# A graph network's streaming stage: target columns read from PSUM, and one PSUM region for the third norm's transposed sums

## What is computed

```python
loop = jnp.arange(n)
row_f = jnp.concatenate([row, loop]); col_f = jnp.concatenate([col, loop])
ew_f = jnp.concatenate([edge_weight, jnp.ones((n,))])
deg = segment_sum(ew_f, col_f, num_segments=n)
dinv = jnp.where(deg > 0, rsqrt(deg), 0.0)
norm = dinv[row_f] * ew_f * dinv[col_f]
out = segment_sum((x @ conv_w)[row_f] * norm[:, None], col_f, num_segments=n) + conv_b
x = layernorm(x + out)
```

## Time and profile before

| | us |
|---|---|
| median of 3 runs | 4627.14 |
| lowest, highest | 4626.38, 4638.19 |
| the profiled execution | 4627.41 |
| its span in the trace | 4625.4 |
| streaming stage in it (first spread at 3134.1, last sums in `acc` at 3461.2) | 327 |

### The profile page before, as it was taken

How to read it: one execution, slowest core, us unless ns; L and a number is a source line. 1 busy time by engine, 2 the same in 40 slices (tenths; PEclk the granted TensorE clock), 3 DMA queues, 4 the chain that set the end, 5 groups by cost and what they waited for, 6 DMA issues and landing times.

```text
span 4625.4 us, 66668 instructions
## 1 busy us (share of the span) xinstructions
PE 3383.2 (73%) x22549; PEld 2235.1 (48%) x22549; DVE 2339.7 (51%) x5589; ACT 1342.3 (29%) x3152; POOL 2432.0 (53%) x2486
## 2 busy tenths in 40 slices
PE   4988888886677766774333333337878999999998
PEld 3654545544455444543223232237874555555554
DVE  7755555555566655655555555557881121111112
ACT  1333233232222222223444444447771000000000
POOL 5777777775777777776777777772330000000000
PEclk7999999998888888886555555558999999999999
DMA  4343334443333333334777777778877777777776
GB/s 127 117 132 121 123 122 133 134 126 104 97 100 93 101 101 100 102 98 133 199 198 199 198 199 198 199 199 321 286 255 289 287 284 276 275 290 283 285 286 227
DMA packets 510752, 855.11 MB, mean 185 GB/s; under 512 B 111438, under 2 KB 290298, under 8 KB 510309
## 3 DMA queue, kind: packets, MB, share of 16 engines
q1 hardware_dynamic: 343350, 542.83, 33.4%
q0 software_dynamic: 87808, 179.98, 15.3%
q10 hardware_dynamic: 79248, 127.90, 7.6%
HBM read 632.93 MB, written 217.55 MB: 184 GB/s over the span
## 4 chain that ended last, share of the span: by engine, by line
POOL 49%; PE 31%; issue 16%; DMA 1%; ACT 1%; DVE 1%; ACTq 0%; POOLq 0%; SPq 0%; DVEq 0%
POOL big L853 32%; POOL big L877 16%; PE psS L1945 11%; PE psA L1945 11%; PE psS L1596 4%; PE psA L1825 1%; PE ps L1891 1%; PE ps L1882 1%; ACT big L1279 1%; PE ps L1526 1%; DMA big<-A_rows 0%; PE psA L1631 0%; PE ps L1465 0%; PE ps L1668 0%; DMA xw_rows<-big 0%
## 5 line engine op out<-in xcount | busy, mean ns | idle before, releaser
L853 POOL DMA_INDIRECT big<-ht_rows,reli x784 | 785.4, 1002 | 269.8 <-issue 238.6
L853 POOL DMA_INDIRECT big<-xw_rows,srci x784 | 775.2, 989 | 271.3 <-issue 238.7
L877 POOL DMA_INDIRECT big<-axt_rows,srci x784 | 746.5, 952 | 262.3 <-issue 238.5
L1596 PE MATMUL psS<-big 128*128 128x128 f32 x3136 | 507.8, 330 | 300.8 <-DMA big<-ht_rows,reli 291.2
L1596 PEld LDWEIGHTS psS<-big 128*128 128x128 f32 x3136 | 476.5, 240 | 368.9 <-DMA big<-ht_rows,reli 326.8
L933 POOL TENSOR_TENSOR xsb<-xsb,l3b2r 128x896 f32<-128x896 f32 x6 | 12.5, 2078 | 1114.4 <-DMA xsb<-x_keep 1114.4
L1945 PE MATMUL psS<-big,xsb 128*128 128x448 f16 x1372 | 485.2, 354 | 17.4 <-DMA big<-A_rows 17.4
L1945 PE MATMUL psA<-big,xsb 128*128 128x448 f16 x1372 | 485.1, 354 | 0.0
L1945 PE MATMUL psS<-big,acc 128*128 128x448 f16 x1372 | 483.8, 353 | 0.0
L1945 PE MATMUL psA<-big,acc 128*128 128x448 f16 x1372 | 483.8, 353 | 0.0
L1757 PE MATMUL ps<-identh,xsb 128*128 128x128 bf16 x784 | 101.4, 311 | 513.8 <-DVE xsb L2444 513.8
(11 more groups left out here) (301 smaller groups left out, 5067.3 us busy)
## 6 DMA issues: line engine op xcount, KB each, us to landing
big<-A_rows SPq DMA_DIRECT2D x112, 2744.0 KB
A_rows<-xsb ACTq DMA_DIRECT2D x196, 416.0 KB, 2.7
xg_rows<-big SPq DMA_DIRECT2D x98, 512.0 KB, 3.8
big<-xg_rows SPq DMA_DIRECT2D x98, 512.0 KB, 4.0
marks_rows<-big SPq DMA_DIRECT2D x98, 354.0 KB
big<-marks_rows SPq DMA_DIRECT2D x98, 354.0 KB, 5.6
big<-srcq_list SPq DMA_DIRECT2D x98, 256.0 KB
ht_rows<-big ACTq DMA_DIRECT2D x28, 512.0 KB, 3.0
```

The costliest lines, as they stand in the source:

```text
L853: pool.indirect_dma_start(ring[g % len(ring)][:, j * D:(j + 1) * D], None, table[:, :], bass.IndirectOffsetOnAxis(ap=lists[:, g * TPG + j: ...
L877: pool.indirect_dma_start(wide[g % NS][:, j, :], None, axt_rows[:, :], bass.IndirectOffsetOnAxis(ap=srci[:, g * TPG + j:g * TPG + j + 1], ...
L1596: m = pe.matmul(psS[b][:, 0:P], rows[b][:, j * P:(j + 1) * P], marks[b][:, j * P:(j + 1) * P], start=(j == 0), stop=(j == TPG - 1))
```

## The change

Four edits. ACT copies `dstf` once into `ps4[:, 1024:1808]`, between the last clearing of degree sums and the loop, after a wait on `d_v`. DVE waits for that copy before its loop, and its marks take the targets from the copy instead of from `dstf`; node numbers still come from SBUF. The transposed sums of all chunks now lie in `ps4[:, 0:896]`, so that `turn_own(c)` waits until chunk c-1, not c-2, has been normalised. `turned_rows(c)`, used in a branch that this input does not take, keeps the two regions under a new name.

```diff
-        def own_sums(c):
+        own_sums = ps4[:, 0:CW]
+        targets = ps4[:, 1024:1024 + NG * TPG]
+
+        def turned_rows(c):
             return ps4[:, c % 2 * 1024:c % 2 * 1024 + CW]
...
             zero_degrees(NCE - 1)
+            act.wait_ge(d_v, 3)
+            act.copy(targets, dstf[:, :]).then_inc(k_ready, 1)
...
             def turn_own(c):
-                if c >= 2:
-                    pe.wait_ge(n_xn, c + (N3["xn0"] - 1))
+                if c:
+                    pe.wait_ge(n_xn, c + N3["xn0"])
                 pe.wait_ge(n_st, c + (N3["xn0"] + 1))
                 for k in range(CB):
-                    m = pe.transpose(own_sums(c)[:, k * P:(k + 1) * P], stT[:, k * P:(k + 1) * P], ident[:, :])
+                    m = pe.transpose(own_sums[:, k * P:(k + 1) * P], stT[:, k * P:(k + 1) * P], ident[:, :])
...
+            dve.wait_ge(k_ready, 4)
+
             def row_marks(b, base, w, pair):
                 dve.tensor_tensor(tiles(marked[b]), iota[:, window(base, w)].unsqueeze(1).broadcast_to([P, TPG, P]),
-                                  columns(dstf, pair, b), ALU.is_equal).then_inc(r_oh[b], 1)
+                                  columns(targets, pair, b), ALU.is_equal).then_inc(r_oh[b], 1)
...
-                step(dve.tensor_tensor(blocks(y[:, :]), blocks(own_sums(c)), per_node(dinv[:, c * CB:(c + 1) * CB]), ALU.mult))
+                step(dve.tensor_tensor(blocks(y[:, :]), blocks(own_sums), per_node(dinv[:, c * CB:(c + 1) * CB]), ALU.mult))
```

More of the change, by code:

```diff
@@ L1283, in turned_back @@
                 act.wait_ge(N3["t2"], c + 1)
-                act.copy(acc[:, c * CW:(c + 1) * CW], own_sums(c)).then_inc(N3["eva"], 1)
+                act.copy(acc[:, c * CW:(c + 1) * CW], turned_rows(c)).then_inc(N3["eva"], 1)
             def store_rows(c):
@@ L1840, in turn_final @@
                 for k in range(CB):
-                    m = pe.transpose(own_sums(c)[:, k * P:(k + 1) * P], X[:, c * CW + k * P:c * CW + (k + 1) * P], ident[:, :])
+                    m = pe.transpose(turned_rows(c)[:, k * P:(k + 1) * P], X[:, c * CW + k * P:c * CW + (k + 1) * P], ident[:, :])
                 m.then_inc(N3["t2"], 1)
```

## The result

| | before | after |
|---|---|---|
| median of 12 runs, us | 4627.80 | 4619.42 |
| lowest, highest | 4621.32, 4638.19 | 4612.39, 4624.60 |
| span of the profiled execution | 4625.4 | 4616.8 |
| first copy of sums at | 3144.95 | 3147.93 |
| from the first to the last copy of sums (98 copies) | 315.25 | 302.93 |

The ratio is 0.9977, with a 95% interval of 0.9969 to 0.9986: 0.23% faster. By the medians that is 8.4 us, by the means (4629.2 and 4618.8) 10.4, where 15.7 were forecast.

What follows compares the result with a forecast made beforehand. DVE, PE and ACT take turns at being late in the streaming stage, with ACT gapless in undisturbed groups. 14.2 + 1.5 = 15.7 us off 4627.41 gave 4611.7 us; range 4606 to 4624, a gain of 3 to 21.

Steps and rivals of the forecast that it cites:

- The bound: Streaming stage: ACT works without a gap at 2.53 us a group, DVE has some 0.2 us reserve; other groups took longer.
- The lock on the marks: DVE's marks wait for POOL instructions, 19.6 us beyond the median; 5.4 hidden, so removing it saves 14.2 us.
- The masks: ACT's staging copy and PE's seven transposes lengthen slots anyway, hiding 2.3 and 1.4 us of the long marks.
- The mark's own duration: DVE's mark with targets in PSUM: 1217 ns against 1216, taken as nothing, within +/-1 us in all.
- The copy, the wait and the single region: ACT's added copy, DVE's wait for it and PE's wait before its transposes: cost nothing.
- One long instruction stays: DVE's L2556, two SBUF inputs, still meets POOL's L893 in chunk 3; no size given.
- PE's clock: Third norm, chunks 1 and 4: shorter pauses without long marks shorten PE's slow two-slot stretches, 1.5 us.
- right: Signs: marks' mean 1210 to 1225 ns, longest below 1300, slots behind L893 2.5 us, stage 13 to 18 us shorter.
- hidden: Sign of a wrong forecast: marks are short, but the stage shortens by less than 10 us.
- More is hidden than I see: Rival, chance 0.14: half of the 14.2 us in the stage is lost, the clock gives nothing; 4620 us.
- The lock did not stay: Rival, chance 0.06: DVE's marks still hold the second port, or POOL stops their write; 4627 us.
- PSUM did not slow the marks: Rival, chance 0.06: the repeated PSUM column makes DVE's marks slower; at 0.5 us a mark, 4647 us.

Runs made afterwards that it cites:

- x_region: The changed kernel with its marks reading dstf from SBUF again, copy and single region kept; 4624.4 us, ratio 0.9995 to the kernel before.
- x_before2: The kernel before, run again with no edit; 4630.1 us, ratio 1.0003.
- x_after2: The changed kernel, run again with no edit; 4618.6 us, ratio 0.9980 to the kernel before.
- x_one_later: The changed kernel with only chunk 1's own_scaled step of POOL one group later; 4614.1 us, ratio 0.9967 to the kernel before.
- x_tiny_sbuf: The kernel before with POOL's three steps cut from 896 columns to 7, so the result is not right; 4608.5 us, ratio 0.9966.
- x_shift2: The changed kernel with POOL's three steps per chunk moved away from the third norm, run a second time; 4610.7 us, ratio 0.9960 to the kernel before.
- x_shift: The changed kernel with POOL's three steps per chunk moved to where DVE has no third-norm piece; 4609.9 us, ratio 0.9965 to the kernel before.

## Why the prediction was right or wrong

**The bound** was read rightly. Undisturbed groups stayed at 2.51 to 2.55 us; what shrank were long ones.

**The lock on the marks: right, and its size nearly so.** DVE's marks lost 138.7 - 118.6 = 20.1 us, of which 19.6 were named. Outside the third norm's busy slots (21 to 25, 35 to 37, 49, 50, 63, 64, 77, 78, 91, 92, and the first) the other 80 slots shrank by 14.2 us together, where I had put 11.4 of the term, with 2.8 in the third norm's. That this equals the whole term is chance. The 19 of the 80 slots that had held a long mark shrank by 10.5 us; the other 3.7 came from slots without one, 1.25 of it from slot 94, which comes up again below. The masks were mostly as read: slot 72, which a staging copy stretches, had a mark 0.72 us too long and lost nothing of its 3.32; slot 30 went from 3.62 to 3.32, slot 75 from 3.68 to 3.00. (The long marks are 22, not 21: the last of all, at 3456.2, took 1478 ns beside a POOL add; its slot was 1.78 us and is 1.79.) One mask was read too large: the slots of PE's transposes that I had at 3.25 us without a long mark (33, 61 and 89) fell to 3.00 too.

**The mark's own duration: right.** 1211 ns for the 1216 before; the earlier trace rows had 1217. The 65 ns of the prediction's estimate from the Trainium skill do not show.

**The copy, the wait and the single region: right**, nothing that shows, by x_region.

**"One long instruction stays": this step failed.** I had looked for DVE's two-input instructions that could meet POOL, and found L2556. It stayed, at 2.49 us. L2311, now L2317, with one SBUF input, was not on the list, since it took 0.17 us in every instance of the first trace. It takes 1.5 to 1.9 us when POOL gets there first. The second trace of the unchanged kernel shows one too, so the change did not make this collision possible:

```profile
3358.02 2.09 POOL L899 TENSOR_TENSOR big<-xsb,cbr 128x896 f32<-128x896 f32 x1
3358.23 1.91 DVE L2311 TENSOR_SCALAR stat<-stat 128x7 f32<-128x7 f32 x1
```

In chunk 0 it goes with PE's clock. Where PE's first group after the norm's pause ran low and the second at full speed, the copy behind which POOL's L889 stands came early enough to fall on L2317: the two traces of the changed kernel and x_region, three of three. In the two traces of the kernel before the second group ran low and the copy came later: in the first, POOL started L886 at 3211.93, when L2311 was over. Slots 21 to 25 grew by 1.8 us instead of losing the 0.7 of slot 24's long mark: 2.5 us off the forecast. In chunk 3 it met POOL in x_before2, x_region, x_after2 and x_one_later, where slots 63 and 64 took 11.8 us together, and not in the first traces of the two kernels, where both groups ran low and these slots took 13.5.

**PE's clock, 1.5 us: this term failed.** I had read 10.4 us for chunk 2's two slots and taken it for what an undisturbed pause gives. The runs without any collision say otherwise. In x_tiny_sbuf all six pairs take 11.9 to 12.0 us, in x_shift2 too; in x_shift three take 10.4 and three 11.7 to 11.9. A pair takes 10.4 if the lower clock falls on the first group, where PE's slowness lies beside DVE's norm work, and some 12 if it falls on the second.

The larger fault is that the pair was cut off too early. Behind a pair of 10.4 us the second slot from there is long, and behind one of 12 it is not. Copies 90, 92 and 94 (chunk 5), before and after:

```profile
3435.93 0.27 ACT L1318 COPY xTs<-psS 128x128 f32<-128x128 f32 x1 [0.39 <-PE psS L1596]
...
3446.42 0.27 ACT L1318 COPY xTs<-psS 128x128 f32<-128x128 f32 x1 [0.86 <-PE psS L1596]
...
3452.78 0.27 ACT L1318 COPY xTs<-psS 128x128 f32<-128x128 f32 x1 [0.75 <-PE psS L1596]
```

```profile
3426.09 0.27 ACT L1324 COPY xTs<-psS 128x128 f32<-128x128 f32 x1
...
3438.09 0.27 ACT L1324 COPY xTs<-psS 128x128 f32<-128x128 f32 x1 [2.38 <-PE psS L1602]
...
3443.20 0.25 ACT L1324 COPY xTs<-psS 128x128 f32<-128x128 f32 x1
```

The pair went from 10.49 to 12.00 us, but the four slots only from 16.85 to 17.11, since slot 94 fell from 3.75 to 2.50. The three pairs of 10.4 in x_shift belong to four slots of 16.7, the six pairs of x_shift2 to four of 17.1: which group runs low is worth 0.3 to 0.4 us, not 1.6. What the term had hoped for, the end of the two-group slow stretches, came in chunk 4, and there four slots lost 1.41 us (18.52 to 17.11), its mark's own 1.37. In chunk 1 the pair fell from 12.84 to 12.10, but the first PE records of the group behind it still ran low, slot 37 rose from 2.66 to 3.56, and the four slots went from 18.08 to 18.17, though a mark 0.74 us too long was gone; in x_after2 they took 17.10. So the term was worth next to nothing. (Its own sum is also off by a little: the middle of 0.1 and 3.1 is 1.6.)

All in all the 17 slots left out above grew by 1.9 us where 4.3 were to be saved, which with the other 80 makes the stage's 12.3.

**From 12.3 or 10.9 to 8.4 us.** The stage's gain is larger than the medians' 8.4 and 8.8; the means give 10.4 for the first measurement. The prediction's signs are half met: the marks, POOL's adds and the slot behind L893 came as written for "right", but the stage shrank by less than the 13 to 18 us named there and by more than the 10 named for "hidden". The interval of the first ratio, 0.9969 to 0.9986, spans 6.5 to 14.3 us and holds both. Twelve traces put the first copy anywhere from 3136 to 3151, in code that is the same up to there but for the added copy; that hides 2 or 3 us of one stage. Whether something of the gain is really given back ahead of the stage stays open; what the runs show is that two executions of one program differ by twice that.

**The rivals.** "More is hidden than I see" comes nearest by its number (4620; measured 4619.4) and is wrong by its mechanism: in the ordinary slots 10.5 us of the 11.4 came. The lock did not stay, and PSUM did not slow the marks.

## What to carry to other kernels

A DVE instruction whose maximum is far above its median, beside POOL work, is worth looking at one by one: move one of its two SBUF inputs to PSUM, or move POOL's instruction to where DVE has nothing that it can hold. When one such collision is removed, list every DVE instruction that POOL could then meet, small single-input ones within SBUF included, and give each a place by the written order: here that was worth another 4 to 8 us of the stage. A term that rests on which group the lower clock falls on needs more than one trace, or none of it belongs in the sum; and it is read to the slot where both courses agree again, not to the end of the two slots where they differ most.

## What the runs showed of the hardware

- A DVE instruction of 128 x 7 elements within SBUF, 0.17 us alone, took 1.51 and 1.91 us when it came 0.20 us behind a POOL instruction of 1.69 and 2.09 us. With its output in PSUM it took 0.17 us, 0.20 us behind one of 2.09 (one instance).
- A DVE input from PSUM in which each column is repeated 128 times costs nothing: 1209 to 1214 ns for 1024 elements a partition, median 1211, against 1216 in the median with both inputs in SBUF.
- Two executions of the same program put the start of one stage 6 us apart after 3.1 ms of the same instructions, while that stage itself repeated within 0.3 us before the change, 1.2 after it and 2.3 with POOL's steps moved.
- Within SBUF the wait goes both ways: a POOL add that began while DVE's long mark was under way took 1.28 us and ended 0.32 us after it, where adds average 0.47 us once the marks read from PSUM.
